# Four tiles' logits and balancing inside the last attention, which goes by halves of batches

## What is computed

```python
x_norm = x * rsqrt(mean(x * x, axis=-1) + RMS_EPS)
H_res = sinkhorn_log((x_norm @ W_res.T).reshape(B, T, 4, 4) + H_res_base)   # 50 iterations, tau 0.1
H_pre = softmax(x_norm @ W_pre.T + H_pre_base)
H_post = softmax(x_norm @ W_post.T + H_post_base)
H_res = (1 - g) * I + g * H_res                                            # g = sigmoid(gate)
y = einsum('btnc,btn->btc', streams, H_pre) @ W_branch
out = einsum('btij,btjc->btic', H_res, streams) + einsum('btc,btn->btnc', y, H_post)
```

## Time and profile before

| | us |
|---|---|
| median of 3 runs (lowest, highest) | 1507.81 (1503.71, 1510.55) |
| the profiled execution, whole | 1506.91 |
| its span, first to last instruction | 1505.2 |
| mean granted TensorE clock | 0.952 of full |
| TensorE, VectorE, ScalarE, GpSimd busy | 89%, 75%, 45%, 23% |
| fourth attention, 30 units with all parts | 930 to 1371 |
| last units and logits | 1371 to 1397 |
| balancing | 1397 to 1479 |
| mixing, copies out, stores | 1479 to 1505 |

### The profile page before, as it was taken

How to read it: one execution, slowest core, us unless ns; L and a number is a source line. 1 busy time by engine, 2 the same in 40 slices (tenths; PEclk the granted TensorE clock), 3 DMA queues, 4 the chain that set the end, 5 groups by cost and what they waited for, 6 DMA issues and landing times.

```text
span 1505.2 us, 18648 instructions
## 1 busy us (share of the span) xinstructions
PE 1345.6 (89%) x6492; PEld 966.2 (64%) x6492; DVE 1123.2 (75%) x2045; ACT 677.1 (45%) x1405; POOL 339.4 (23%) x380
## 2 busy tenths in 40 slices
PE   8999999999998989977999998999999999999105
PEld 5665566566575648736888875777777777777102
DVE  4788898888888996976555576666666566568998
ACT  4778777877433443432222224443434444443104
POOL 1112122212164020233111021312222212213620
PEclk9999999999999999988999998999999999999557
DMA  5678888788810011323211210101101101000001
GB/s 218 170 179 184 226 225 197 173 221 213 224 43 1 1 57 34 79 64 79 71 42 42 96 71 1 71 28 43 71 29 43 69 13 61 1 1 1 0 0 56
DMA packets 37910, 127.74 MB, mean 85 GB/s; under 512 B 4944, under 2 KB 10960, under 8 KB 31680
## 3 DMA queue, kind: packets, MB, share of 16 engines
q1 hardware_dynamic: 26304, 83.38, 16.0%
q0 software_dynamic: 11520, 43.26, 15.1%
HBM read 72.63 MB, written 10.75 MB: 55 GB/s over the span
## 4 chain that ended last, share of the span: by engine, by line
PE 57%; DVE 23%; DVEq 6%; ACT 6%; DMA 4%; issue 2%; POOL 1%; POOLq 1%; SPq 0%
PE PS L150 12%; PE PS L152 11%; PE PS L151 11%; DVE AR L676 5%; PE PS L925 4%; PE PS L963 4%; DMA AR<-AR 3%; ACT s_sb L606 2%; DVE AR L2601 2%; PE PS L949 2%; DVE AR L2590 2%; DVE AR L2597 2%; DVEq L666 2%; DVE AR L682 1%; PE PS L535 1%
## 5 line engine op out<-in xcount | busy, mean ns | idle before, releaser
L438 POOL DMA_DIRECT2D AR<-AR x76 | 75.7, 1127 | 334.4 <-DMA AR<-AR 133.5
L151 PE MATMUL PS<-R16r 128*128 128x512 f32 (+1 forms) x328 | 122.1, 372 | 0.0
L535 PE MATMUL PS<-R,PT 128*128 128x512 f32 x256 | 116.1, 596 | 3.7 <-DVE X L716 3.7
L510 PE MATMUL PS<-R,HT 128*128 128x256 f32 x512 | 116.5, 381 | 3.2 <-ACT R L595 3.1
L152 PE MATMUL PS<-R16r 128*128 128x512 f32 (+1 forms) x312 | 119.1, 382 | 0.0
L510 PEld LDWEIGHTS PS<-R,HT 128*128 128x128 f32 x512 | 94.8, 190 | 16.2 <-ACT R L595 4.6
L1083 ACT COPY AR<-PS 128x512 f32<-128x512 f32 x64 | 37.5, 586 | 146.1 <-PE PS L152 145.7
L606 ACT ACTIVATE s_sb<-PS,sm 128x64 f32<-128x64 f32 x256 | 78.2, 338 | 53.4 <-DVE sm L701 52.8
L150 PE MATMUL PS<-HTr,R16r 128*128 128x512 f32 (+1 forms) x240 | 90.7, 378 | 4.6 <-DVE R16r L190 2.5
L150 PE MATMUL PS<-R16r,HTr 128*128 128x512 f32 (+1 forms) x224 | 90.2, 403 | 0.0
L152 PE MATMUL PS<-HTr,R16r 128*128 128x512 f32 (+1 forms) x240 | 87.7, 365 | 0.0
(11 more groups left out here) (313 smaller groups left out, 3495.0 us busy)
## 6 DMA issues: line engine op xcount, KB each, us to landing
AR<-AR POOLq DMA_DIRECT2D x76, 528.0 KB, 6.7
OR<-in_wo SPq DMA_DIRECT2D x12, 1024.0 KB, 12.4
dequantised<-AR SPq DMA_DIRECT2D x8, 1056.0 KB, 5.5
WR<-in_w0q SPq DMA_DIRECT2D x8, 1024.0 KB, 11.5
AR<-in_w3q SPq DMA_DIRECT2D x8, 1024.0 KB, 4.9
WR<-dequantised SPq DMA_DIRECT2D x22, 256.0 KB, 2.8
AR<-in_nf SPq DMA_DIRECT2D x4, 1056.0 KB, 9.4
nf_in<-in_nf SPq DMA_DIRECT2D x4, 1056.0 KB, 10.6
```

The source lines that it names most:

```text
L151: nc.tensor.matmul(out, ah, bl, start=False, stop=False)
L438: nc.gpsimd.dma_start(nf_below(g)[:, part], what[:, part], accum_op=ALU.add, max_dma_last_dim=4 * N_NF // 2).then_inc(added, 16)
L510: i = nc.tensor.matmul(bank(2 + u % 2)[:, tt * 256:(tt + 1) * 256], HT0[:, c, tok], m[:, :, c * B + b, :], start=c == 0, stop=c == C - 1)
L535: i = nc.tensor.matmul(bank(5 + tt), PT[:, at:at + P], vo[:, pr, b, :], start=pr == 0, stop=pr == 1)
```

## The change

1. **The fourth attention by halves of batches.** Groups are now 16 (`NG3`) of two batches (`BH`): units 0 to 15 run all eight key/value heads for batches 0 and 1 (tiles 0 to 3), units 16 to 31 for batches 2 and 3. Keys and values, their norm and their turning are made 16 times at half width; all weights of the attention are loaded twice, and split twice by ScalarE and GpSimd, now in every unit.
2. **The last stage in two halves h of four tiles.** Tiles 0 to 3 are turned in units 16 and 17, with bank 4 for it, and their logits follow in unit 18. Rows, columns and kernel matrices of half 0 are made in units 18 to 21.
3. **Balancing inside the attention.** From unit 22 on, `between(n)` stands behind VectorE's instructions and issues up to n steps of half 0. Half 0's kernel matrices lie in SBUF; those of half 1 stay in PSUM.
4. **The rest.** Behind the attention the steps of half 1 alternate with what is left of half 0 (`both`). Half 0's mixing, by ScalarE and TensorE, runs beside half 1's balancing; at the end VectorE mixes tiles 4 and 5, ScalarE and TensorE 6 and 7.
5. **Second attention and what follows it.** Projections go by halves, one or two in each unit. GpSimd's two large splits go by four parts, each behind a `probs` of VectorE. In `pool_f1` the accumulating transfers and the scaling of the second weights (`pool_f2(pool, (1,))`) come later; VectorE normalises tiles 2 and 3 of the third feed-forward ahead of the statistics (`dve_stats`) of tiles 4 to 7.

```diff
+        TH = T // 2
+        PIECES3 = 6
+        VO_AT = (1, 4)
+        BH = B // 2
+        NG3 = 2 * NG
+        KH = BH * SK
+        def batch3(u):
+            return u // NG3 * BH + u % BH
...
+                if u in (NG3, NG3 + 1):
+                    pe_turn7(pe, 2 * (u - NG3))
+                if u == NG3 + 2:
+                    pe_logits(pe, 0)
                 if more:
                     turn_q(u + 2, 1)
                 outputs(u, 1)
...
                 if u + 1 < NU0:
                     exps(u + 1)
+                if u in (NG3, NG3 + 1):
+                    act_norm(act, 7, (2 * (u - NG3),))
                 if more:
                     query_row(u + 2, 1)
                     query_turned(u + 2, 0)
...
+            def between(n=1):
+                if balancing[0]:
+                    f3.balance(0, n)
...
+                balancing[0] = u >= NG3 + 6
+                between()
                 if u + 1 < NU0:
                     shift(u + 1)
+                between(2)
                 probs_low(u)
+                between(2)
                 if more:
                     square_sum(u + 2, 0)
+                between(2)
                 if u + 1 < NU0:
                     norm(u + 1)
+                between(2)
...
                     folded_low(vg, vb, 0)
+                between(2)
                 add(u, 0)
+                between(2)
...
+                between(2)
                 add(u, 1)
+                between(2)
                 if vg < NG3:
                     folded_low(vg, vb, 1)
+                between()
...
+        KP = (at3(10880 + 480, TH * NM), bank(6)[:, 0:TH * NM])
+        KT = (at3(10880 + 544, TH * NM), bank(6)[:, TH * NM:2 * TH * NM])
...
+            def balance(self, h, n):
+                for _ in range(min(n, self.limit[h] - self.done[h])):
+                    part = self.done[h] % ROUND
+                    k, given, got = (KP[h], CC[h], RR[h]) if part < 3 else (KT[h], RR[h], CC[h])
+                    self.after_last(h)
...
-            pool_low(Wh[:, 0:C * NWF], Wl[:, 0:C * NWF], WR[:, 0:C * NWF]).then_inc(F1["split"], 1)
+            for c in range(C):
+                cols = slice(c * NWF, (c + 1) * NWF)
+                pool.wait_ge(A1["probs"], NU // 2 + c)
+                pool.wait_ge(F1["w_hi"], c // 2 + 1)
+                i = pool_low(Wh[:, cols], Wl[:, cols], WR[:, cols])
...
+            accumulate(pool, LATE, 2)
             accumulate(pool, LATE, 3)
+            pool.wait_ge(hn_ready, T * 5)
             pool_f2(pool, (1,))
```

More of the change, by code:

```diff
@@ L1513, in pe_a1, with project_q @@
         def pe_a1(pe):
[L1514 to L1515 removed]
+            def project_q(b, pr, halves=(0, 1)):
+                if b and halves[0] == 0:
                     pe.wait_ge(A1["qT_ready"], 2 * b - 1 + pr)
[L1517 to L1519 removed]
+                for hh in halves:
                     hc = 2 * pr + hh
@@ new lines, in pool_f3, with before @@
+            pool_norm_pair(pool, 7, 2)
+            pool_norm_pair(pool, 7, 3)
+            def before(h):
+                pool.wait_ge(F3["post"], h + 1)
+                if h == 0:
+                    pool.wait_ge(A3["shifted"], NU0)
+                for n in range(NS):
+                    dst = XP if n == 0 else XTMP
+                    nc.gpsimd.tensor_tensor(dst.rearrange("p (t c) -> p t c", t=TH), rows7(h)[:, :, n, :],
+                                            tiles(PP[h])[:, :, n].unsqueeze(2).to_broadcast([P, TH, P]), ALU.mult)
+                    pool.drain()
+                    if n:
+                        nc.gpsimd.tensor_tensor(XP, XP, XTMP, ALU.add)
+                        pool.drain()
+                pool.drain().then_inc(F3["pre"], 1)
+                nc.gpsimd.tensor_tensor(PP[h], PP[h], tg[:, 1, 3:4].to_broadcast([P, TH * 2 * NS]), ALU.mult)
+                pool.drain()
@@ new lines, in dve_f3, with both @@
+        def dve_f3(dve, f3):
+            def both(n):
+                for _ in range(n):
+                    f3.balance(1, 1)
+                    if f3.left(0):
+                        f3.balance(0, 1)
+                        if not f3.left(0):
+                            f3.mixing(0)
+            f3.balance(0, 6)
+            scaled7(dve, (6, 7))
+            f3.logits(1)
+            f3.rows(1)
+            f3.balance(0, 3)
+            f3.row_sums(1)
+            f3.balance(0, 3)
+            f3.columns(1)
+            f3.balance(0, 3)
+            f3.column_sums(1)
+            f3.balance(0, 3)
+            f3.shifted_columns(1)
+            f3.balance(0, 4)
+            f3.kernels_ready(1, 7)
+            both(f3.left(1))
+            f3.factors(1)
+            f3.balance(0, 4)
+            f3.refresh(1)
+            f3.balance(0, 4)
+            f3.kernels_ready(1, 10)
+            both(f3.left(1))
+            f3.mixing(1)
+            H3 = tiles(K3[1])
+            dve.wait_ge(F3["posted"], 2)
+            for j in range(NS):
+                for t in (4, 5):
+                    for i_ in range(NS):
+                        xt = X[:, t, i_ * P:(i_ + 1) * P]
+                        nc.vector.scalar_tensor_tensor(xt, hn_of(7, t)[:, j * P:(j + 1) * P],
+                                                       H3[:, t % TH, i_ * NS + j:i_ * NS + j + 1], xt, ALU.mult, ALU.add)
+                if j < NS - 1:
+                    dve.drain()
+            dve.drain().then_inc(F3["done"], 1)
```

945 lines of the change are left out of this document (533 added, 412 removed).

## The result

The changed kernel takes 1539.05 us (median) against 1509.18 for the kernel before beside it: a ratio of 1.0207, with a 95% interval of 1.0184 to 1.0231. That is about 30 us slower (31 by the ratio), where 18 were forecast; the stated range reached to 1542. The profiled execution has a span of 1534.9 us against 1505.2, 29.7 more.

A forecast was written before the change was run, and what follows sets the result against it. TensorE was taken to bound the fourth attention, VectorE's step issue the balancing. Terms -11.5 + 3 + 7.7 + 12 + 8.0 + 11.7 - 1.3 - 2.6 - 8.8 = +18.2 on 1506.9 gave 1525 us; range 1492 to 1542.

The forecast's parts named there:

- Second attention and after: Second attention and the work behind it: VectorE's waits and a slowed multiplication go, later waits shrink; -11.5 us.
- Keys and values by halves: Fourth attention: sixteen half-width groups of keys and values instead of eight, plus turning; +3 us (bounds 0 and +6).
- Units 16 to 18: Fourth attention: turning and logits of half 0 on TensorE's path, plus ScalarE's copies; +7.7 us (bounds +4 and +11).
- term for ScalarE's queue: Units 16 and 17: ScalarE copies the turned tile ahead of copies the query turning needs; 1.6 twice, 3.2 us.
- Steps inside units 22 to 28: Attention: balancing steps delay `folded_low`, which keys and values await, and GpSimd blocks half 0's multiplications; +12 us.
- the clock falls: Rival: stalls of 3 us in the attention lower TensorE's clock, so each costs its length again; +12, 1537 us; chance 0.15.
- End of the attention: Units 30 and 31 and behind: 41 steps cost 7.8, GpSimd blocking 2.5, fewer logits return 2.3; +8.0 us.
- The two phases: Balancing behind the attention: alternating pairs, then singles at 0.25; first phase +11.7, refresh -1.3, second phase -2.6 us.
- The end: Behind the balancing: ScalarE's scalings and the chain to the last copy serve two tiles, not four; -8.8 us.
- The slack takes it: Rival: in units 22 to 28 steps fit VectorE's waits, singles cost 0.22, multiplications miss GpSimd; 1494 us, chance 0.22.
- Nothing is blocked: Rival: GpSimd reads SBUF beside the 64-column steps without holding them; 1507 us, no change; chance 0.15.

The follow-up runs named there:

- Part 5 alone: The kernel before with only the second-attention changes: halved projections, GpSimd's splits in four parts, later accumulating transfers, earlier normalisation; 1498.44 us, ratio 0.9939.

## Why the prediction was right, and where it was not

The sign and the range held, and the mechanism named as the forecast was the one found: steps ahead of an instruction that TensorE waits for, half 0's multiplications held by GpSimd, and single steps that cost as much as pairs. The size came out at +18.2 against +29.7, from terms that were off both ways. At 1539 the time lies at the very edge of the forecast's own range (1515 to 1539).

- **Second attention and after: right**, -11.5 against -10.9. The turning behind the second attention starts at 638.85 instead of 646.62, 7.8 earlier (6 forecast). Of the two waits, 3.96 and 4.08, the first is gone and the second is 1.72, but one in front of the third attention's turning of probabilities grew from 1.72 to 4.48. Part 5 alone gave 9 us.
- **Keys and values by halves:** over units 3 to 14 the cost is nil (177.73 us against 177.35), less than the +3. What was not foreseen is the start of the attention: +4.2 before unit 3, where TensorE's waits sum to 8.1 us against 4.5 (2.6 of the 8.1 for normalised tiles, 4.1 for the folding and 1.4 for the second keys and values, which are now made there).
- **Units 16 to 18: the step that failed most.** "five groups of four logit matmuls at 0.49 (1.96 for 16) are 2.5". A group has eight records, not four: the 16 of rows 9 are two tiles, and the five groups here show 8 and 32. They took 4.78. To that come some 1.2 us of lowered clock behind them, which had no term. The term for ScalarE's queue was right, 3.2 against 3.5. In all 11.9 against 7.7.
- **Steps inside units 22 to 28: mechanism right, size too large.** +12 was the sum, 9.3 the measured price (8.1 and the 1.2 of the wait at 1346.57). The keys and values wait for `folded_low` as said, 1.0 to 1.7 us and not 2.2, and GpSimd's work held four of the multiplications in these units and not six (0.85 at 1275.59 is one). In two of the three pairs the clock added some 1.6 us, at 0.91 over the unit. The rival "the clock falls" is thus true in part and was counted as an alternative: 1.2 in units 16 to 18, 3.3 here and some 2.2 behind the scores of unit 31 (the last by the run without late steps) make an estimated 6 to 7 us of the 30, with no term in the sum. That its 1537 lies nearest the measured time is luck: it had put 12 in the attention alone.
- **End of the attention:** +8.0 against +11.0. That the 22 steps among the logits "stand in waits such as the 1.97 at 1390.93 and cost nothing" failed: they cost 3.4. The 41 of units 30 and 31 cost 4.0, less than their 7.8. The other 3.6 are there without any step. The sum had 0.2 for them, GpSimd's 2.5 less 2.3 for logits of four tiles. What it lacked is TensorE: with half 0's tiles turned long before, it waits for `probs_low` with nothing to do and runs the outputs at the lower clock.
- **The two phases:** the alternating 87 pairs took 32.49 where 33.6 were forecast, half 0's mixing 3.3 (2.2). "I take 0.22 and such a handover, 0.25" failed: a single step costs 0.267, just as the pair does. 57 took 15.2 and 150 took 40.0, 3.4 us more than the sum had. The larger error was to call the pace issue, since the bound 0.22 of the rival rested on it.
- **The end:** -8.8 against -8.7.
- **Rivals.** "The slack takes it" is refuted by the run without steps. It was decided at the point named, whether the low half ends before TensorE needs it, and with six steps moved behind it the slack did take most of them. "Nothing is blocked" is refuted by the matrices in PSUM.

So the change could not pay in its main part. It shortened no chain: half 1's 294 steps of 0.267 us are as long as 294 pairs. Its one true gain, a shorter mixing, is 8.7 us, and part 5 gave 9 to 11 that needed none of it.

## What to carry to other kernels

Where two chains of dependent steps alternate and one alone runs at the same pace, moving one of them elsewhere saves nothing; take half of the steps out of the kernel before, which is a few lines, and see whether the time moves. When small work is put into an engine's idle time, look for the instruction that another engine waits for and put the work behind it: the order cost 6.7 us, and what is left with the steps behind it, against no steps at all, is 2.6 (132.60 against 129.99 from the scores of unit 22 to those of 31). While GpSimd is busy, one of two operands of a small VectorE instruction belongs in PSUM.

## What the runs showed that was not expected

- A single balancing step, executing in 0.21 to 0.25 us, is followed 0.25 to 0.29 us later by the next, and a second chain fits in between for nothing (ratio 1.0002).
- In a TensorE that is otherwise full, waits of 1.72 and 1.59 us in front of the keys were followed by the lower clock, 0.91 over the unit; the eight matmuls behind the first took 2.04 instead of 1.16 us. It is not the wait alone: the same wait of 1.71 to 1.72 was followed by 1.16 at full clock in the run without late steps and in that with the matrices in PSUM, and the two of 1.74 in front of L965 left 1.00 as well. Behind waits of 0.55 and 0.46 the unit stayed at 1.00.
- 4.8 us of matmuls with only 24 columns were followed by the lower clock in the changed kernel, without a wait. In the run with ScalarE's order changed they were not.
- A matmul of 24 columns in float32 has two records of 0.12 us each at full clock (3.73 us for 32, and 1.96 for 16 in the kernel before).
